# Layer 0's recurrence with B and C read from PSUM instead of from ScalarE's copies

## The reference

```python
xd = jnp.einsum('bdl,kd->blk', x, xw)
dts = xd[..., :R_DT]
Bs = xd[..., R_DT:R_DT + n]
Cs = xd[..., R_DT + n:]
delta = jax.nn.softplus(jnp.einsum('blr,dr->bld', dts, dtw) + dtb)
A = -jnp.exp(Al)
xt = x.transpose(0, 2, 1)
dA = jnp.exp(delta[..., None] * A)
dBx = delta[..., None] * Bs[:, :, None, :] * xt[..., None]

def step(h, inp):
    da, dbx, c = inp
    h = h * da + dbx
    return (h, jnp.einsum('bdn,bn->bd', h, c))
```

## Time and profile before

| | |
|---|---|
| runs shown | 19030.96, 19056.55, 19087.31 us |
| median | 19056.55 us |
| profiled execution, first to last instruction (span) | 17337.0 us |
| profiled execution's own time | the page gives no figure beside the span |
| mean granted TensorE clock | 0.734 of full speed |
| recurrence of layer 0, image 0 (no gather beside it) | 391.3 us |
| the same, images 1 to 7 | 534.8 to 542.1 us each |

### The profile page before, as it was taken

The page is one execution under the profiler, slowest core; times in us unless marked ns, Lnnn a source line. Parts: engine busy times, 40 slices in busy tenths (PEclk is TensorE's granted clock), DMA queues, the critical chain, the costliest instruction groups (busy, mean ns, idle before and its releaser), DMA issues. The chain is left out here.

```text
span 17337.0 us, 88370 instructions
## 1 busy us (share of the span) xinstructions
PE 9223.9 (53%) x27936; PEld 4289.2 (25%) x27936; DVE 10031.7 (58%) x9815; ACT 3711.2 (21%) x4683; POOL 10558.2 (61%) x9221
## 2 busy tenths in 40 slices
PE   5761548635675447754486355763567544773004
PEld 2320223212232213322132122322123221331002
DVE  6544855559554675547655485555945467554333
ACT  3320223113220222212231122311222022220000
POOL 0017767368655776467673776746865577647772
PEclk8885678867777678776687667885777767876557
DMA  1011111211122111311112211121112211131111
GB/s 37 8 38 59 33 46 53 76 58 35 50 64 81 36 38 53 80 61 34 43 53 76 63 32 47 51 78 57 35 51 66 79 35 38 54 80 52 53 54 46
DMA packets 903981, 903.34 MB, mean 52 GB/s; under 512 B 692583, under 2 KB 720119, under 8 KB 894264
## 3 DMA queue, kind: packets, MB, share of 16 engines
q0 software_dynamic: 294912, 604.57, 12.2%
q1 hardware_dynamic: 608568, 292.73, 5.9%
HBM read 770.26 MB, written 126.36 MB: 52 GB/s over the span
## 5 line engine op out<-in xcount | busy, mean ns | idle before, releaser
L120 POOL DMA_INDIRECT gat<-corner_table,idx x9216 | 10557.8, 1146 | 6492.1 <-issue 2775.3
L738 PE MATMUL PS<-hc,ident 128*128 128x512 f32 (+2 forms) x4096 | 2022.6, 656 | 1719.7 <-DVE hc L794 1645.4
L146 DVE TENSOR_TENSOR gat<-gat,wts 128x1152 f32<-128x1152 f32 x1024 | 1385.0, 1353 | 2407.1 <-DMA gat<-corner_table,idx 2407.1
L132 DVE TENSOR_REDUCE dcn<-gat 128x32 f32<-128x1152 f32 x1024 | 2167.4, 2117 | 625.0 <-DMA X<-in_x_dram 359.5
L738 PEld LDWEIGHTS PS<-hc,ident 128*128 128x128 f32 x4096 | 951.8, 275 | 2602.2 <-DVE hc L794 2079.0
L829 DVE TENSOR_TENSOR_SCAN hs<-dA,dB 128x1024 f32<-128x1024 f32 (+2 forms) x672 | 1536.0, 2287 | 27.9 <-issue 19.3
L1028 PE MATMUL PS<-kk,q 64*128 64x512 f32 x2048 | 1161.3, 693 | 12.8 <-DVE kk L1149 12.8
L1039 PE MATMUL PS<-ident,E 128*128 128x128 f32 x4096 | 707.4, 329 | 690.8 <-ACT ET L1095 630.6
L1052 PE MATMUL PS<-ET,vo 128*128 128x512 f32 x2048 | 972.6, 631 | 7.1 <-DVE ET L1156 7.1
L1125 ACT ACTIVATE E<-PS,nmax 128x1024 f32<-128x1024 f32 x512 | 570.1, 1113 | 1846.8 <-DVE nmax L1178 1842.0
L1178 DVE TENSOR_REDUCE nmax<-PS 128x1 f32<-128x1024 f32 x512 | 623.3, 1217 | 453.7 <-PE PS L1028 453.0
(11 more groups left out here) (250 smaller groups left out, 11854.0 us busy)
## 6 DMA issues: line engine op xcount, KB each, us to landing
gat<-corner_table,idx POOLq DMA_INDIRECT x9216
corner_table<-xp SPq DMA_DIRECT2D x1024, 64.0 KB, 2.2
D<-in_dist_dram SPq DMA_DIRECT2D x8, 4096.0 KB, 12.3
wqkv<-in_qkv_w_dram SPq DMA_DIRECT2D x8, 3072.0 KB, 10.0
X<-in_x_dram SPq DMA_DIRECT2D x32, 512.0 KB, 5.9
w_in<-in_in_w_dram SPq DMA_DIRECT2D x16, 1024.0 KB, 7.0
w_c<-in_c_w_dram SPq DMA_DIRECT2D x16, 1024.0 KB
keep_scratch<-X SPq DMA_DIRECT2D x8, 2048.0 KB, 11.7
```

The costliest lines, as they stand in the source:

```text
L120: nc.gpsimd.indirect_dma_start(bd.gat[n % NG][:, k * 4 * CG:(k + 1) * 4 * CG], None, bd.io["table"][:], bass.IndirectOffsetOnAxis(ap=bd.id ...
L132: nc.vector.tensor_reduce(bd.dcn[m % 2][:, g * CG:(g + 1) * CG], bd.gat[n % self.NG][:].rearrange("p (k c) -> p c k", c=CG), AX.X, ALU.add)\
L146: nc.vector.tensor_tensor(v, v, wv, ALU.mult).then_inc(self.prod, 1)
L738: mm = nc.tensor.matmul(PS[:, p.ybank(t, d, h), 0:p.hl], self.ident[:], src[:, j, h * p.hl:(h + 1) * p.hl], start=(c == 0 and j == 0), sto ...
```

## The change

ScalarE's copies, `Bs`, `Cs` and their waits are gone. VectorE's `weigh` reads B and `multiply` reads C in PSUM. Each has one place there, so PE writes B of chunk ci+1 when both weightings of chunk ci are done, at the top of the first run of chunk ci, and C of chunk ci+1 when the last product of chunk ci is done. One counter of broadcasts becomes two. Two buffers `r1` take the place of `Bs` as scratch of the stage before. The diff, without the unchanged loop bodies:

```diff
-                Bs = [self.sb(c2, f"Bs{i}", [P, N]) for i in range(2)]
-                Cs = [self.sb(c2, f"Cs{i}", [P, N]) for i in range(2)]
-                self.l0_steps(passes, xw, dtw, (hs, hc), (dA, Bs), dB)
-                self.l0_recurrence(passes, dA, dB, hs, hc, Bs, Cs)
+                r1 = [self.sb(c2, f"r1{i}", [P, N]) for i in range(2)]
+                self.l0_steps(passes, xw, dtw, (hs, hc), (dA, r1), dB)
+                self.l0_recurrence(passes, dA, dB, hs, hc)
...
+        Bp, Cp = (PS[:, 2 * i:2 * i + 2, :].rearrange("p i f -> p (i f)") for i in range(2))
...
             @block.tensor
             def _(pe):
-                def broadcast(ci):
+                def broadcast(ci, which, done):
 
                     p, c = chunks[ci]
-                    for which in range(2):
-                        if ci:
-                            pe.wait_ge(bc_out, 2 * ci - 1 + which)
...
-                        mm.then_inc(bc_done, 1)
-
-                broadcast(0)
-                broadcast(1)
...
+                    mm.then_inc(done, 1)
+
+                broadcast(0, 0, b_done)
+                broadcast(0, 1, c_done)
                 for u, (k, ci, p, c, t, d) in enumerate(runs):
-                    if t == 0 and d == 0 and ci + 2 < len(chunks):
-                        broadcast(ci + 2)
+                    if t == 0 and d == 0 and ci + 1 < len(chunks):
+                        pe.wait_ge(weighed, DT * (ci + 1))
+                        broadcast(ci + 1, 0, b_done)
 
                     pe.wait_ge(hc_ready, u + 1)
+                    if u + 1 == last_run["chunk", ci] and ci + 1 < len(chunks):
+                        broadcast(ci + 1, 1, c_done)
...
             @block.scalar
             def _(act):
-                def copies(ci):
-                    for which, dst in ((0, Bs), (1, Cs)):
-
-                        if ci >= 2 and which == 0:
-                            act.wait_ge(weighed, DT * (ci - 1))
-                        elif ci >= 2:
-                            act.wait_ge(hc_ready, last_run["chunk", ci - 2])
-                        act.wait_ge(bc_done, 2 * ci + which + 1)
-                        nc.scalar.activation(dst[ci % 2][:].rearrange("p (i f) -> p i f", i=2),
-                                             PS[:, 2 * which:2 * which + 2, :], ACT.Copy).then_inc(bc_out, 1)
-
-                copies(0)
...
-                    if t == DT - 1 and ci + 1 < len(chunks):
-                        copies(ci + 1)
...
-                    dve.wait_ge(bc_out, 2 * ci + 1)
+                    dve.wait_ge(b_done, ci + 1)
...
-                    nc.vector.tensor_tensor(p.body(dB[k % 2]), p.shaped(Bs[ci % 2]), src, ALU.mult)\
+                    nc.vector.tensor_tensor(p.body(dB[k % 2]), p.shaped(Bp), src, ALU.mult)\
...
-                    dve.wait_ge(bc_out, 2 * ci + 2)
+                    dve.wait_ge(c_done, ci + 1)
...
-                    nc.vector.tensor_tensor(p.body(hc[u % 2]), p.body(hs[u % 2]), p.shaped(Cs[ci % 2]), ALU.mult)\
+                    nc.vector.tensor_tensor(p.body(hc[u % 2]), p.body(hs[u % 2]), p.shaped(Cp), ALU.mult)\
```

More of the change, by code:

```diff
@@ L686, in _, with l0_recurrence @@
                 spread.end()
-    def l0_recurrence(self, passes, dA, dB, hs, hc, Bs, Cs):
+    def l0_recurrence(self, passes, dA, dB, hs, hc):
         nc, PS = self.nc, self.PS
-        names = "bc_done bc_out da_ready scanned hc_ready y_done y_kept gaps_zero weighed rec_order"
-        bc_done, bc_out, da_ready, scanned, hc_ready, y_done, y_kept, gaps_zero, weighed, order_s = [self.sem(n) for n in names.split()]
+        names = "b_done c_done da_ready scanned hc_ready y_done y_kept gaps_zero weighed rec_order"
+        b_done, c_done, da_ready, scanned, hc_ready, y_done, y_kept, gaps_zero, weighed, order_s = [self.sem(n) for n in names.split()]
+        Bp, Cp = (PS[:, 2 * i:2 * i + 2, :].rearrange("p i f -> p (i f)") for i in range(2))
         chunks = [(p, c) for p in passes for c in range(p.chunks)]
@@ L726, in _ @@
-                broadcast(0)
-                broadcast(1)
+                    for i in range(2):
+                        per = max(1, NH // p.L)
+                        for j in range(per):
+                            n = c * p.nn + (i * per + j if p.nn > 1 else 0)
+                            row = which * NS + n
+                            pos = slice(0, p.L) if p.nn > 1 else slice(i * NH, (i + 1) * NH)
+                            mm = nc.tensor.matmul(PS[:, 2 * which + i, j * p.hl:(j + 1) * p.hl],
+                                                  self.pick[:, row:row + 1].to_broadcast([3 * BC, P]),
+                                                  p.bc[:, pos], start=True, stop=True)
```

## The result

The changed kernel takes 19481.85 us (median of 4 runs, 19451.57 to 19517.66) against 19071.93 us (19030.96 to 19094.93, 4 runs) measured beside it: ratio 1.022, 95% interval 1.0201 to 1.0239, or 410 us slower. The forecast was slower, 19360 us within 19030 to 19720.

A forecast was written before the change was run, and what follows sets the result against it. The prediction took VectorE to bound the recurrence, with GpSimd's indirect DMAs as second bound in later images. First image +132 and seven later ones +175 gave +307 us, added to a 19056.55 us median: 19360 us, range 19030 to 19720.

The forecast's parts named there:

- The start of the recurrence, -3 us: At each recurrence's start, without ScalarE's copies the exponentials begin sooner: -3 us an image, between -1 and -3.4.
- VectorE's operations cost 0: VectorE's 158 operations a stage that now read one operand from PSUM take as long as before: 0, 18 us either way.
- S: Weighting's wait for PE's chain of C, sum into y, then B: 3.1 us fast, 5.6 slow, 4.35 taking half and half.
- Image 0, +132: First recurrence, no gather beside it: 31 waits of 4.35 us make 135, less 3 at the start: +132 us.
- 19 places in full and 12 with a unit between, +97 a later image: Later recurrences: 19 weightings wait 4.35 us, 12 wait 1.15 because a gathered unit hides the rest: +97 us.
- Gather waits, -37: In later recurrences GpSimd gets ahead, so 37 of VectorE's 40.6 us of waiting for gather transfers go.
- Tail, -32: VectorE's idle gap after a later recurrence, while GpSimd issues its last transfers, shrinks from 40.3 to 8.1 us: -32.
- Their cause: GpSimd relieved in later recurrences: two-SBUF-operand work falls from 428 to 237 us; VectorE's new waits also leave it free.
- A later image, +25 us: Each of seven later images: +97 of waits, -3 at the start, -37 gather waiting, -32 end gap: +25 us.
- Rival 1: PE at 1.2 GHz at nearly every broadcast, each wait 5.6 us: +605 us, 19660 us; chance 0.18.
- Rival 2: Faster: GpSimd's returned time outweighs a short wait, at least 2.7 us: -64 us, 18990 us; chance 0.07.
- Rival 4: GpSimd not relieved by PSUM reads, gather waits and end gap stay: +790 us, 19850 us at most; chance 0.05.

The follow-up runs named there:

- the square: Four kernels, copies or PSUM operands, each without and with the added wait; image 2's recurrence: 537.6 and 609.6 us with copies, 517.7 and 603.7 with PSUM.
- B in time: Changed kernel, but PE writes B of chunk ci+2 before its wait for chunk ci's last product; 17182.21 us, ratio 0.9921 to the kernel before.
- B before the sum: Changed kernel, but PE writes B of chunk ci+2 right behind C of ci+1, ahead of the sum into y; 17257.56 us, 0.9963 of the kernel before.
- the wait in the kernel before: Kernel before, with ScalarE's copy of B also waiting for the sum into y, all VectorE operands staying in SBUF; 19515.95 us.

## Why the prediction was right, point by point

- **The start of the recurrence, -3 us.** The exponentials start at 192.05, the first scan at 196.06, 3.96 us after the stage's start instead of 7.03: -3.1. Right.
- **VectorE's operations cost 0.** 1219 to 1221 and 1195 ns from PSUM against 1217 to 1221 and 1200 from SBUF. Right. The Trainium skill (VectorE: DVE Perf Modes, the TRN2 errata) has 62 cycles more for an operation that reads PSUM, an estimated 65 ns. The trace does not agree: the means lie within 5 ns of each other.
- **S = 4.35 us.** It measured 4.68. The places were right, so was the chain. The step that failed in a small way is "I take half and half": the clock does not change at random from place to place. C and y ran at 1.2 GHz and B at 2.4 at nearly all places, so S is neither 3.1 nor 5.6 but one value between. That it lies so near the mean of the two is luck: half and half was taken without a row.
- **Image 0, +132.** +148. The waits at the 31 places add up to 141.7 us instead of 135. In the pass with 256 positions, where the prediction put 0 and at most 4 us, there is one wait of 6.3 us and two of 1.0: the longest has 16 sums of the pass before in front of B (6.93 us on PE).
- **19 places in full and 12 with a unit between, +97 a later image.** There are 19 and 12, at 4.7 to 5.1 and at about 1.45 us (none at one of them), 106.7 us together; with the two in the short pass 111.4 (163.0 us of waits less the 51.6 that stand before the stage's first weighting). The gap is mostly the size of S again.
- **Gather waits, -37.** They fell to 0.0, -40.6. **Tail, -32.** -25.8: 14.5 stay, not 8.1. "The last unit may be issued only after VectorE's last sum" was too early: that sum ends at 4865.97, but GpSimd was still issuing the unit before it, until 4870.6. And VectorE was through 7.2 us behind that sum, not 9.0.
- **Their cause.** Here the argument failed although the size held: "the weightings and products by C no longer have two operands in SBUF" was named first, the idle VectorE second. By the square, the idle time does it alone, and the freed operands alone give 17 us of gather waits and nothing of the tail. That the 37 us held all the same is no merit of the argument: only 40.6 us of gather waits were there to lose, and the idle time took them all. What the prediction priced wrongly is the stretch of two-operand work, 428 us going to 237, as if each microsecond freed were won: GpSimd issues two transfers in most steps either way, as long as the scan stays. GpSimd's mean in the stage fell from 1612 to 1423 ns, not towards 1300. The rule of the Trainium skill (SBUF — State Buffer, Who interferes with whom) agrees with the traces in direction, 1550 ns going to 1485 with B in time.
- **A later image, +25 us.** +40 by the trace (65.7 - 25.8). **The sum, +307.** By the stages 148 + 7 x 40 = 428; the medians differ by 410 and 458 on two pairs, and the 95% intervals, 383 to 456 and 421 to 489, both hold the 428. So the medians leave nothing over that the noise does not cover. The forecast's own band, S from 3.5 to 5.2, comes by its terms to some 19155 to 19565, not 19120 to 19520.
- **Rival 1** (PE at 1.2 GHz nearly everywhere, +605) was right of the clock, 0.66 and 0.63, and wrong of its price: the last link, B, ran at 2.4. **Rival 2** (faster) names the point S = 3.1 from which it decides; the kernel with S taken down to 1.13 to 1.98 and the one without it are indeed faster, 0.9963 and 0.9921. **Rival 4** fell with the tail. The prediction set a faster kernel on a faster clock; what it takes is another place for one broadcast.
- **The 10% between span and runs.** "Nothing I read says where": it was another chip, as far as the record shows (below), and adding the difference to the runs' median was the right use of it.

## What to carry to other kernels

When a copy between two engines goes, ask what the copy decoupled: here not the data but the order, since one buffer less puts the writer behind everything that stands ahead of it in its own queue. Write the single buffer at the first point in the writer's order at which its reader is done with it, ahead of waits for other work; the same operands in PSUM then gain 0.8% instead of losing 2.2%. And where two engines alternate as the bound, the idle time that a new wait makes is not all lost, and work moved across a stage's border is only gained if the bound engine has room on the other side.

## What the runs showed of the hardware

**Chips differ by a tenth on this kernel.** Before took 17320.1 us (14 runs, within 0.1%) on one chip, 19045.95 and 18972.02 on two others. Each chip was used in one session, so chip and session can't be told apart. The kernel with B in time has a profile from the first and the third, with the same recurrences (517.7 and 517.5 us in image 2), and spans of 17180.6 and 18806.9 us. The line that differs, over the whole run, first chip and third:

```profile
L1167 DVE TENSOR_REDUCE nmax<-PS 128x1 f32<-128x1024 f32 x512 | 623.2, 1217 | 447.6 <-PE PS L1017 447.1
```

```profile
L1167 DVE TENSOR_REDUCE nmax<-PS 128x1 f32<-128x1024 f32 x512 | 624.5, 1220 | 1483.0 <-remote 728.7 <-PE PS L1017 585.4 <-issue 168.3
```

It is attention's maximum: the operation takes as long on both, but 1035 us more of idle time stand before its 512 instances, part of it with nothing in the profile to name ("remote"). That is not all: of the 1626 us between the two spans, 965 lie in attention's layer and 562 in layer 3, whose copies of a row (L1638) stand idle 1206 us before their start on the first chip and 1681 on the third. What the chips do otherwise in these layers is open. Comparisons of two spans are only good on one chip, or stage by stage.

**The granted clock fell with the waits.** With the same matmuls, the first recurrence ran at a granted 0.80 with B in time (1.6 us of waits at the weightings), 0.77 with B before the sum (41 us), 0.66 in the changed kernel (152 us) and 0.64 with the wait in the kernel before (153 us). The sums into y, which took 1.82 us at 2.4 GHz and 3.39 at 1.2 GHz in before, take 3.32 at nearly all places of the changed kernel, and they are a part of the wait. So more waiting went with a lower clock, and the lower clock made the wait longer.

**What holds up an indirect DMA.** One that starts with a weighting takes 2.01 us with both operands in SBUF, or 4.15 where the scan behind holds it too, and 0.95 with B in PSUM. One held by a scan ends 0.75 us behind it, beside a product of either kind.
